# Transformer block with a sixteen-tile attention stage: weight unpacking dealt out in pieces, scores in twelve of sixteen steps, maxima transposed earlier

## What is computed

```python
x = x + gamma * attention0(layernorm(x), ctx, ctx)   # 8 heads over the 256 positions as channels, 32 per head, length 512
x = x + ffn_fp4(layernorm(x))                        # gate_up and down weights packed as 4-bit floats, rms norm
x = x + attention1(layernorm(x), ctx)                # 16 heads, int8-like rounding of q, k, v and weights
x = x + ffn_ternary(layernorm(x))
```

## Time and profile before

| | us |
|---|---|
| three runs | 1996.06, 2001.64, 2005.15; median 2001.64 |
| profiled execution, its own time | 2005.03 |
| its span in the profile | 2003.3 |
| mean granted clock of TensorE | 0.956 of full |
| first stage (`mix_rows`) | 0 to 398 of the span |
| from transposition of step 0 to that of step 14 | 59.30 to 371.61 |

### The profile page before, as it was taken

One profiled execution on the slowest core, in us unless ns is written; L12 is line 12 of the kernel. 1 busy time (PEld: TensorE's weight loads), 2 busy tenths in 40 slices (PEclk: granted clock), 3 DMA queues, 4 the chain that ended last, 5 costly groups with the idle time before them and its releaser, 6 DMA issues. The chain is left out here.

```text
span 2003.3 us, 32495 instructions
## 1 busy us (share of the span) xinstructions
PE 1776.8 (89%) x11262; PEld 789.5 (39%) x11262; DVE 1588.8 (79%) x2930; ACT 1230.9 (61%) x2011; POOL 916.8 (46%) x935
## 2 busy tenths in 40 slices
PE   3987998779999969948899999999999979579998
PEld 1322222234444434524444444444444434234443
DVE  5889999677767758886799999999999965784433
ACT  4876786445544414423489999999999974322111
POOL 5565666246445410020068888888888870000000
PEclk9999999989999989978999999999999989799999
DMA  9753561121000011100044555455556554000000
GB/s 209 199 141 90 129 154 32 29 85 22 2 21 22 1 63 37 31 6 26 0 90 106 107 110 107 106 107 110 108 107 106 110 104 177 6 0 22 21 21 21
DMA packets 334720, 147.54 MB, mean 74 GB/s; under 512 B 290544, under 2 KB 306928, under 8 KB 333424
## 3 DMA queue, kind: packets, MB, share of 16 engines
q1 hardware_dynamic: 334576, 145.70, 31.4%
HBM read 70.15 MB, written 4.19 MB: 37 GB/s over the span
## 5 line engine op out<-in xcount | busy, mean ns | idle before, releaser
L1564 ACT ACTIVATE a_prob<-a_psS,a_bias,q_scale 128x1024 uint8<-128x1024 f32 x512 | 610.2, 1212 | 28.5 <-PE a_psS L1457 24.6
L1493 DVE TENSOR_REDUCE a_tops<-a_psM 128x1 f32<-128x512 f32 x1024 | 622.5, 678 | 2.1 <-PE a_psM L1447 0.6
L1543 POOL CAST a_wide<-a_pairs 128x2048 int16<-128x2048 uint8 x256 | 481.4, 1894 | 98.7 <-DMA a_pairs<-a_prob 83.8
L1447 PE MATMUL a_psM<-KT,QO 128*128 128x512 bf16 x1024 | 371.3, 387 | 5.9 <-PEq L1241 2.2
L1457 PE MATMUL a_psS<-KT,QO 128*128 128x512 bf16 x1024 | 306.5, 381 | 3.1 <-ACT a_prob L1564 3.0
L1469 PEld LDWEIGHTS a_psO<-V,a_wide 128*128 128x128 f16 x4096 | 175.1, 96 | 147.0 <-DVE QO L1506 23.0
L483 ACT ACTIVATE prob<-psT 128x512 f32<-128x512 f32 x256 | 145.8, 612 | 101.6 <-PE psT L690 100.9
L1469 PE MATMUL a_psO<-V,a_wide 128*128 128x32 bf16 x4096 | 181.6, 177 | 21.2 <-DVE QO L1506 15.6
L847 DVE SCALAR_TENSOR_TENSOR g_sum<-g_psG,gu_scale,g_sum 128x512 f32<-128x512 f32 x176 | 124.1, 745 | 89.9 <-PE g_psG L999 75.2
L825 POOL TENSOR_TENSOR g_sum<-g_sum 128x512 f32<-128x512 f32 x88 | 126.5, 1438 | 140.3 <-DVE g_sum L847 140.3
L548 DVE TENSOR_REDUCE rmax<-psS 128x1 f32<-128x512 f32 x256 | 161.8, 669 | 28.9 <-PE psS L676 28.7
(11 more groups left out here) (211 smaller groups left out, 2872.8 us busy)
## 6 DMA issues: line engine op xcount, KB each, us to landing
xs<-in_x SPq DMA_DIRECT2D x64, 256.0 KB, 7.5
cs<-in_ctx SPq DMA_DIRECT2D x64, 256.0 KB, 8.9
KT<-in_w SPq DMA_DIRECT2D x2, 4096.0 KB, 21.1
raw_gu<-in_gu SPq DMA_DIRECT2D x4, 1408.0 KB, 9.4
vs<-in_ctxT SPq DMA_DIRECT2D x16, 256.0 KB, 3.0
k_cT<-in_ctxT SPq DMA_DIRECT2D x16, 256.0 KB, 2.6
a_pairs<-a_prob SPq DMA_TRANSPOSE x256, 2.7
out<-x_sb SPq DMA_DIRECT2D x16, 256.0 KB, 2.0
```

The lines of the kernel that those rows point to most:

```text
L1447: pe.matmul(psM[n % NM][:, :], QOf[:, i * P:(i + 1) * P], KTf[:, keys:keys + 512], start=True, stop=True).then_inc(shown, 1)
L1493: v.reduce_max(tops[i // JOIN % NB][:, i % JOIN, c:c + 1], psM[n % NM][:, :], AX.X).then_inc(topped, 1)
L1543: pool.tensor_copy(wide[i % NV][:, :, :, :].rearrange("p k c q -> p k (c q)"), both).then_inc(widened, 1)
L1564: act.activation(prob[i % NP][:, k * HK:(k + 1) * HK], psS[g % NS][:, :], ACT.Exp, scale=q_scale[:, i:i + 1], bias=bias[i // JOIN % NB][:, ...
```

## The change

The unpacking is dealt out: a slice of 704 columns (`PER` = 4 to a group, 16 slices k in all) is done with its three instructions at n = 6, 10 and 13 of one step, one slice in each of steps 3 to 14, the rest at the ends of steps 14 (one) and 15 (two) and in step 15 (one). The scores of the next tile are done in n = 0 to 11, two of them at n = 1, 4, 7 and 10, both on TensorE and, with their maxima, on VectorE. VectorE's `split` moves to n = 12 and the second of the mid-step statistics to n = 13, the last reciprocal to n = 14. TensorE's `turn_maxima` comes ahead of `weigh(j, 2)`. GpSimd waits, between the two halves of `queries(j + 2)`, for the `split` of the tile before. The third load of packed weights moves from step 9 to step 8.

```diff
-    UP = 2
-    INVERT, STATS = (5, 7, 9, 11), (1, 3)
-    UNPACK = (4, 5, 6, 7, 11, 12, 13, 14)
-    FETCH_GU = (2, 3, 9, 11)
-    UW = 2 * FI // (2 * UP)
+    INVERT, STATS = (5, 8, 11, 14), (2, 13)
+    UNPACK = {j: (j - 3,) for j in range(3, NT - 2)}
+    UNPACK.update({NT - 2: (11, 12), NT - 1: (13, 14, 15)})
+    BITS = (6, 10, 13)
+    SCORES = [1 + (n in (1, 4, 7, 10)) if n < 12 else 0 for n in range(NU)]
+    FIRST_SCORE = [sum(SCORES[:n]) for n in range(NU)]
+    FETCH_GU = (2, 3, 8, 11)
+    PER = 4
+    UW = 2 * FI // PER
...
                     if g >= 2:
-                        sp.wait_ge(bits_s, 6 * UP * (g - 1))
+                        sp.wait_ge(bits_s, 3 * PER * (g - 1))
...
                 for h in range(HT):
                     pool.wait_ge(q_cut, 2 * j + h // 2 + 1)
+                    if h == HT // 2 and has(j - 1):
+                        pool.wait_ge(parts_ready, j)
...
+            def unpack(k, i):
+                g, at = k // PER, slice(k % PER * UW, (k % PER + 1) * UW)
+                words = raw_gu[:, g % 2, at]
+                if i == 0:
+                    v.wait_ge(gu_loaded[g], 16)
+                    move_bits(v, env, words).then_inc(bits_s, 1)
+                if i == 1:
+                    v.wait_ge(bits_s, 3 * k + 1)
+                    keep_bits(v, words).then_inc(bits_s, 1)
+                if i == 2:
+                    v.wait_ge(bits_s, 3 * k + 2)
+                    v.tensor_scalar(env["w_gu"][:, g, at], words.bitcast(F32), 2.0 ** 126, None,
                                     ALU.mult).then_inc(bits_s, 1)
...
                 for n in range(NU):
-                    if has(j + 1):
-                        greatest(j + 1, n)
+                    for i in range(SCORES[n] if has(j + 1) else 0):
+                        greatest(j + 1, FIRST_SCORE[n] + i)
+                    if n == 12 and has(j + 1):
+                        split(j + 1)
                     if n in INVERT and has(j - 1):
                         invert(j - 1, INVERT.index(n))
                     if n in STATS and has(j + 3):
                         statistics(j + 3, STATS.index(n))
-                    if n == NU // 2 and j in UNPACK:
-                        unpack(UNPACK.index(j))
-                if has(j + 1):
-                    split(j + 1)
+                    if n in BITS and j in UNPACK:
+                        unpack(UNPACK[j][0], BITS.index(n))
...
+                for k in UNPACK[j][1:] if j in UNPACK else ():
+                    for i in range(len(BITS)):
+                        unpack(k, i)
...
                     if has(j):
                         tscore(j, n)
-                    if has(j + 1):
-                        score(j + 1, n)
+                    for i in range(SCORES[n] if has(j + 1) else 0):
+                        score(j + 1, FIRST_SCORE[n] + i)
                     if has(j) and n in WEIGH:
                         weigh(j, WEIGH.index(n))
-                if has(j):
-                    weigh(j, 2)
                 if has(j + 1):
                     turn_maxima(j + 1)
                 if has(j):
+                    weigh(j, 2)
                     weigh(j, 3)
```

## The result

The changed kernel takes 1967.78 us (four runs, 1967.22 to 1971.55) against 2000.18 us before in the same comparison. The ratio is **0.9841, 95% interval 0.9814 to 0.9867**: 1.6% faster. The prediction said 1976 us, with a range of 1962 to 1992.

What follows compares the result with a forecast made beforehand. VectorE (steps with unpacking) and TensorE alternate as limits. Terms of +1.6, -20.5 and -8.3 sum to -27.2 us from the profiled 2005.0, giving 1977.8, or 1974.4 for the median; forecast 1976, range 1962 to 1992.

Steps and rivals of the forecast that it cites:

- VectorE's sum of 19.2 is the floor of a step with unpacking: Steps with one slice: VectorE's work is 19.2 us against TensorE's 18.7; as a rival, about 1963 us, chance 0.13.
- Plain steps pay for the doubled scores: Steps 1 and 2: doubled scores outrun three banks, 20.0 us each, together +1.0; step 0 +0.6.
- The waits behind GpSimd: Steps with unpacking: first unpacking instruction waits 0.75 us for GpSimd's `ks`, second 0.3 for its `qs`; bounds 0 and 0.96.
- The transposition no longer waits: End of each unpacking step: `split` and TensorE's four `tscore` both end at 16.48 us, so TensorE's 2.77 us wait goes.
- Steps 13 and 14: No statistics there, so the first bank wait goes: 19.9 and 19.6 us, 39.5 against 47.77, -8.3.
- GpSimd's new wait costs nothing: GpSimd's wait for `split` in `queries`: `split` ends at 16.5 us, ScalarE's second `q_sub` cut later; no cost.
- Step 15 costs nothing: Step 15's three slices lie in VectorE's idle time before the last reciprocals; no cost.
- The start: Start-up ahead of step 0's first `tscore`: the forecast's sum had no term for it.
- full waits behind GpSimd: Rival: all three unpacking instructions of a step meet GpSimd; steps 21.5 to 22 us, about 1991 us, chance 0.12.
- Slower, mrow late: Rival: VectorE over 1.1 us late with `mrow` for the next step, TensorE idles, clock falls; about 2015 us, chance 0.05.
- The total: First stage: steps 0 to 2 +1.6, 3 to 12 -20.5, 13 and 14 -8.3, together -27.2 us.

Runs made afterwards that it cites:

- experiment 7: The changed kernel with the three unpacking instructions of a slice at n = 9, 12 and 13 instead of 6, 10 and 13: 1966.00 us.
- experiment 11: The changed kernel with unpacking at n = 9, 12, 13, one step 15 slice moved to step 14, and reciprocals and statistics at other n: 1955.41 us.
- experiment 5: The changed kernel without GpSimd's wait for `split` between its pairs of queries: 1967.47 us, ratio to the kernel before 0.983.
- the first two expectations: Ratios expected for the kernel before with only unpacking dealt out, about 0.992 (measured 1.010), and with only the order changed, about 0.994 (measured 1.0057).
- experiment 1: The kernel before with only the unpacking dealt out, scores in all sixteen n and no wait on GpSimd: 2020.78 us, ratio 1.010.
- experiment 4: The kernel before with the unpacking dealt out and GpSimd's wait for `split`, scores still in all sixteen n: 1973.75 us, ratio 0.9871.
- experiment 12: The kernel before with GpSimd's wait, scores in all sixteen n, unpacking dealt out at n = 9, 13, 14, one slice moved to step 14: 1969.05 us.

## Why the prediction was right, step by step

- *VectorE's sum of 19.2 is the floor of a step with unpacking.* Right in kind, 0.2 us too dear: in experiment 7 VectorE's rows show 0.62 us of idle time in 19.59, which leaves 19.0; experiment 11 comes down to 19.13.
- *Plain steps pay for the doubled scores.* Right in kind and too dear: 19.59 instead of 20.0 laid out. The two bank waits are there, 0.38 and 0.60 us. Step 1 rose from 18.69 to 19.59, but step 2 fell from 20.31: before, TensorE waited 1.27 us in it for ScalarE's `prob`, which it does not do after (why is not shown). Steps 0 to 2 cost 0.2 us and not 1.6.
- *The waits behind GpSimd.* Each was mis-sized: 0.75 for the first, measured near 0 in six steps and 0.94 to 1.02 in four, 0.41 on average; 0.3 for the second, measured 0.57 to 0.97, 0.71 on average. Together they are 1.1 a step, as laid out, which is luck. The sum for the ten steps, 205.0, was 2.3 us above the measured 202.7. Two errors cancel in part: without waits behind GpSimd ten steps take 195.9 (experiment 7) where the layout had 200, 4.1 too dear, and with them they take 6.8 more where the layout had 5.0, 1.8 too cheap.
- *The transposition no longer waits.* Nearly: 0.17 to 0.57 us ahead of L722 in steps 3 to 12.
- *Steps 13 and 14.* 38.3 measured, 39.5 laid out.
- *GpSimd's new wait costs nothing.* Right (experiment 5); in step 9 the slack is 2.4 us, `split` ending at 234.15 and ScalarE's cut at 236.56.
- *Step 15 costs nothing.* Wrong by 1.5 us: the slices at its end meet GpSimd, take 7.5 us, and the last four reciprocals start at 358.04 instead of 356.51.
- *The start.* Not in the sum: -2.5 us. At start-up a statistic waits for its load with maxima queued behind it; two more maxima now run ahead of it and the second statistic stands behind `split`, which takes 1.8 us off that path. The other 0.7 is the arrival of the load (28.81 against 29.54); that the change moved it is not shown.
- The rival *full waits behind GpSimd* happened in part, in four steps of ten. *Slower, mrow late* did not: in step 9 VectorE has `mrow` at 237.1, TensorE needs it at 238.2.
- *The total.* -33.0 where the sum had -27.2: 1.4 us from steps 0 to 2, 2.3 from steps 3 to 12, 1.1 from steps 13 and 14 and 2.5 from the start, less 1.5 for step 15.

What the prediction did not see is how the parts hang together. It priced them one by one as gains and small losses, and so did the first two expectations, which both missed for it. Alone, either part leaves TensorE with gaps of 2.8 to 5.4 us, and most of these cost the clock as well.

By the Trainium skill (SBUF — State Buffer, section "Who interferes with whom") whichever of the two engines starts first blocks the other for its whole instruction, and a VectorE `tensor_tensor` with two SBUF inputs contends with a GpSimd instruction that reads SBUF. The traces agree: in experiment 1 the 128 x 16 `tensor_tensor` L564 takes 1.07 us, and 0.18 in experiment 4 (L566 there), where GpSimd idles; and the third `ks` of the changed kernel shows GpSimd as the one that waits. A chain of dependent little instructions pays once for each: 0.51 + 0.90 + 1.02 us in experiment 1.

## What to carry to other kernels

Where two engines hold each other up, look first at the short dependent chain that a third engine waits for: beside the dealing, one wait that keeps `split` off GpSimd was worth 46 to 47 us, more than the whole change. Place a bulky instruction by what stands behind it in its queue: the same run of six cost 40 us more ahead of the maxima than behind `split`. And try the parts of a change alone before crediting any: here two losses of 0.6 and 1.0% made a gain of 1.6%.

## What the runs showed of the hardware that was not expected

TensorE's idle gaps of 2.8 to 5.4 us in steps 3 to 14 were nearly all followed by a weighing at half the rate, in whole or in part: up to 1.94 + 1.94 us for rows that otherwise take about 1.07 + 1.04. The one exception is the first gap of experiment 1, 3.17 us at 119.61, behind which the weighing takes 1.07 + 1.04. The view of TensorE's clock by stretch, for experiment 1, has the weighing behind the gap of 3.17 us (above, at 241.84) and a stretch of the next step; the last three columns are the granted clock, the DMA share, and GB/s:

```profile
242.07:245.64 3.57, 3.57 (x17) 0.59 (x17) 2.47 (x8) 0.00 (x0) 1.08 (x2) 0.50 0.00 0
257.00:262.00 5.00, 4.49 (x27) 1.44 (x28) 5.00 (x7) 4.33 (x8) 2.28 (x2) 1.00 0.01 2
```

That is 1.2 GHz for the weighing and 2.4 GHz again afterwards. Gaps of 1.1 us, one in each of steps 3 to 13 of experiment 12, and single ones of 1.57 (experiment 1, 364.96) and 1.81 us (experiment 12, 336.88) were followed by weighings of full rate.

The wait behind GpSimd settled into two kinds of steps, 19.82 and 20.94 us, which mostly came several in a row: a few hundredths of a us between L745 and GpSimd's third `ks` make 1.1 us of difference. Experiment 5, the same kernel but for a wait that is always passed already, had them in another arrangement: five short ones (3 to 7), then five long ones (8 to 12).
